# One core, sixteen sequences through two transformer blocks: an explicit turn for every piece of work, one copy for the values, and a mask term on another engine

## The reference

```
# block 0 (per sequence)
x = x + Wo·attention(q,k,v of LN(x), mask_self)            # 16 heads of 16
x = x + Wc·attention(q of LN(x), k,v of ctx, mask_cross)
x = x + W2·gelu(W1·LN(x))
# attention: scores = (q·k)/4 * mask - 10000*(1 - mask); softmax; times v
# block 1 (per sequence): recurrent mixing, 32 heads of 8
xn = LN(x); sx = shift(xn) - xn; five mixed streams from a low-rank tanh
w = exp(-exp(...)); per token: s = k v^T + w*s; out = r·(u k v^T + s)
x = x + (groupnorm(out) * silu(g))·Wo
x = x + sigmoid(r2) * relu(k2)^2·Wv
```

## Time and profile before

| | |
|---|---|
| time, median of 3 runs | 693.77 us (692.63 to 694.01) |
| span of the profiled execution | 694.0 us |
| PE busy | 645.3 us (93%) |
| DVE busy | 598.2 us (86%) |
| ACT busy | 571.7 us (82%) |
| POOL busy | 311.6 us (45%) |
| mean granted TensorE clock | 0.985 |

### The profile page before, as it was taken

One profiled execution on the slowest core, in us unless ns is written; L12 is line 12 of the kernel. 1 busy time (PEld: TensorE's weight loads), 2 busy tenths in 40 slices (PEclk: granted clock), 3 DMA queues, 4 the chain that ended last, 5 costly groups with the idle time before them and its releaser, 6 DMA issues.

```text
span 694.0 us, 17297 instructions
## 1 busy us (share of the span) xinstructions
PE 645.3 (93%) x5877; PEld 561.6 (81%) x5877; DVE 598.2 (86%) x1430; ACT 571.7 (82%) x2071; POOL 311.6 (45%) x440
## 2 busy tenths in 40 slices
PE   6878998999999999999999999999999989898776
PEld 5666787888989888988989888989888877687555
DVE  3598588999999999999999999999999987968274
ACT  1568899899999999999999999999999987664513
POOL 1154252646464554636364646454554624432120
PEclk9999999999999999999999999999999999999799
DMA  8920031221305050504122231305050503120200
GB/s 306 325 70 9 2 104 36 70 70 58 88 9 138 1 146 1 145 2 122 25 85 62 67 81 53 93 4 144 1 146 1 146 0 108 31 70 0 69 9 8
DMA packets 53725, 50.44 MB, mean 73 GB/s; under 512 B 6030, under 2 KB 48902, under 8 KB 53254
## 3 DMA queue, kind: packets, MB, share of 16 engines
q1 hardware_dynamic: 53638, 49.34, 24.7%
HBM read 28.62 MB, written 3.93 MB: 47 GB/s over the span
## 4 chain that ended last, share of the span: by engine, by line
PE 80%; DVE 8%; ACT 7%; issue 3%; POOL 1%; DMA 0%; SPq 0%; DVEq 0%; ACTq 0%; POOLq 0%
PE PS_B L552 16%; PE PS_T L654 9%; PE PS_B L694 8%; PE PS_S L552 7%; PE PS_D L559 5%; PE PS_S L625 4%; PE PS_T L662 4%; PE PS_S L559 4%; PE PS_T L559 4%; ACT SC L1291 3%; PE PS_D L800 2%; PE PS_B L703 2%; PE PS_D L552 2%; ACT PT L1301 2%; PE PS_T L545 2%
## 5 line engine op out<-in xcount | busy, mean ns | idle before, releaser
L1291 ACT ACTIVATE SC<-SC,NMX 128x128 f32<-128x128 f32 x512 | 200.0, 398 | 0.2
L1291 ACT ACTIVATION_READ_ACCUMULATOR SC<-SC,NMX 128x1 f32 x512 | 101.0, 197 | 0.0
L654 PE MATMUL PS_T<-CST,SC 128*128 128x128 f32 x512 | 81.3, 281 | 7.7 <-ACT PT L1301 3.6
L976 DVE TENSOR_REDUCE NMX<-SC 128x4 f32<-128x512 f32 x128 | 85.2, 676 | 0.4 <-POOL SC L1499 0.3
L1301 ACT ACTIVATE PT<-PS_T 128x512 f32<-128x512 f32 x120 | 70.8, 590 | 12.7 <-PE PS_T L654 12.7
L654 PEld LDWEIGHTS PS_T<-CST,SC 128*128 128x128 f32 x512 | 56.4, 141 | 26.1 <-ACT PT L1301 12.7
L1057 DVE TENSOR_TENSOR_SCAN SS<-W,AJ 128x1024 f32<-128x1024 f32 x32 | 73.2, 2288 | 0.2
L552 PE MATMUL PS_B<-MX,W 128*128 128x128 f32 x512 | 64.2, 280 | 4.7 <-ACT KR L1350 4.7
L552 PEld LDWEIGHTS PS_B<-MX,W 128*128 128x128 f32 x512 | 61.3, 196 | 4.9 <-ACT KR L1350 4.9
L1499 POOL TENSOR_TENSOR SC<-SC,MADD 128x512 f32<-128x512 f32 x48 | 59.9, 1276 | 6.5 <-DVE SC L956 6.5
L552 PE MATMUL PS_B<-B_LT,W 128*128 128x128 f32 x512 | 61.1, 278 | 1.0 <-ACT B_LT L1231 0.9
(11 more groups left out here) (231 smaller groups left out, 1595.0 us busy)
## 6 DMA issues: line engine op xcount, KB each, us to landing
W<-EW SPq DMA_DIRECT2D x32, 512.0 KB, 4.1
V<-values_by_head SPq DMA_DIRECT2D x28, 512.0 KB, 5.4
W<-in_weights SPq DMA_DIRECT2D x1, 4160.0 KB, 21.0
ENC<-in_enc SPq DMA_DIRECT2D x16, 128.0 KB, 2.3
out<-X SPq DMA_DIRECT2D x16, 128.0 KB, 5.8
X<-in_x SPq DMA_DIRECT2D x1, 1920.0 KB, 15.7
values_by_head<-VC SPq DMA_DIRECT2D x14, 128.0 KB, 1.8
W<-in_weights SPq DMA_DIRECT2D x1, 1280.0 KB, 8.5
```

The lines of the kernel that those rows point to most:

```text
L654: last = pe.transpose(PS_T[:, j * T:(j + 1) * T], SC[:, nr(b, a) % 2, g, j, :], ident)
L976: dve.tensor_reduce(NMX[:, nr(b, a) % 2, GH * g:GH * g + GH], SC[:, nr(b, a) % 2, g], AX_X, ALU.max, negate=True)\
L1291: last = act.activation(SC[:, nr(b, a) % 2, g, j, :], SC[:, nr(b, a) % 2, g, j, :], ACT.Exp, bias=NMX[:, nr(b, a) % 2, h:h + 1], accum_out ...
```

## The change

1. `run` no longer walks a list cycle by cycle. Each entry has a turn number in ten-thousandths of a cycle (TURN = 10000); a piece of sequence b has the place TURN*b + turn, and each engine's pieces are sorted by it. A second table per engine (`PE_MOVED`, ...) gives single sequences of a piece a turn of their own. So every engine's order is new, and it need not repeat from one sequence to the next.
2. `a_val` copies both halves by one ACTIVATE through a strided view, `halves(n)`.
3. `a_lessmask` moves from ACT to POOL, as a `tensor_scalar` with multiply and add.

How far the orders move, by comparing the lists: of PE's 800 pieces 565 keep their place and the mean shift is 0.4 places (9 at most); of DVE's 1408, 465 keep it, mean shift 1.8 (24 at most); of ACT's, mean shift 1.9 (35 at most); of POOL's, 2.6. On SP the stores of the results come two cycles later than before, behind the DMAs of the decays and values.

```diff
-    ("d_final", 0, 6), ("a_addmask", (0, 0), 1), ("b_addnorm", 0, 4), ("b_addnorm", 1, 4), ("b_addnorm", 2, 4),
...
+    ("a_root", 0, 4880), ("a_addmask", (0, 0), 9189), ("a_addbias", 0, 13591), ("a_addmask", (0, 2), 14279),
+    ("a_lessmask", 0, 20510), ("a_root", 1, 22743), ("a_addbias", 1, 24972), ("a_addmask", (1, 0), 25421),
...
+def in_order(order, moved):
+    turns = [(TURN * b + moved.get((name, arg), {}).get(b, turn), name, arg, b)
+             for name, arg, turn in order for b in range(B)]
+    return [(name, arg, b) for _, name, arg, b in sorted(turns, key=lambda t: t[0])]
...
+        def halves(n):
+            whole = VP[:, n]
+            return bass.AP(whole.tensor, whole.offset, [whole.ap[0], [4 * HD, NH // 2], [3 * HD, 2], [1, HD]])
...
-        def run(pieces, order, i):
-            for name, arg, lag in order:
-                if 0 <= i - lag < B:
-                    pieces[name](i - lag, arg)
+        def run(pieces, order, moved):
+            for name, arg, b in in_order(order, moved):
+                pieces[name](b, arg)
...
-                v = values.rearrange("p (h q d) -> p h q d", q=2, d=HD)
-                for q in range(2):
-                    last = act.activation(VP[:, nr(b, a) % 2, :, q, q * HD:(q + 1) * HD], v[:, :, q, :], ACT.Copy)
-                last.then_inc(a_v, 1)
+                act.activation(halves(nr(b, a) % 2), values.rearrange("p (h q d) -> p h q d", q=2, d=HD), ACT.Copy)\
+                    .then_inc(a_v, 1)
...
-            def a_lessmask(b, _):
-                if not later(b):
-                    act.wait_ge(in_rest, IN_REST)
...
-                act.activation(MADD[:, b % 2, :], MASK[:, b, :], ACT.Copy, bias=-10000.0, scale=10000.0)\
-                    .then_inc(a_less, 1)
...
+            def a_lessmask(b, _):
+                if not later(b):
+                    pool.wait_ge(in_rest, IN_REST)
+                if b > 1:
+                    pool.wait_ge(a_added, nth(POOL_ADDS, b - 2, max(POOL_ADDS)))
+                    pool.wait_ge(a_dadded, nth(DVE_ADDS, b - 2, max(DVE_ADDS)))
+                pool.tensor_scalar(MADD[:, b % 2, :], MASK[:, b, :], 10000.0, -10000.0, ALU.mult, ALU.add)\
+                    .then_inc(a_less, 1)
```

More of the change, by code:

```diff
@@ L84 @@
     ('d_keyrec', 0, 15): 4, ('d_val', 0, 15): 2}
+TURN = 10000
 SP_ORDER = [
-    ("b_vspread", 0, 4), ("d_store", 0, 6), ("b_wspread", 0, 3), ("b_vstore", 0, 3), ("a_load", 0, 0)]
-PE_ORDER = [
[L90 to L99, removed]
@@ L133 @@
-POOL_ORDER = [
-    ("d_final", 0, 6), ("a_addmask", (0, 0), 1), ("b_addnorm", 0, 4), ("b_addnorm", 1, 4), ("b_addnorm", 2, 4),
[L135 to L140, removed]
+    ("a_load", 0, 90000), ("b_wspread", 0, 110004), ("b_vstore", 0, 110008), ("b_vspread", 0, 120002),
@@ new lines @@
+    ("d_store", 0, 170032),
+]
+SP_MOVED = {
+    ("b_wspread", 0): {0: 120002, 1: 110008}, ("b_vstore", 0): {0: 120004, 1: 110010}, ("b_vspread", 0): {0: 120006},
+}
+PE_ORDER = [
+    ("a_turn", 0, 5843), ("a_key", 0, 7175), ("a_val", 0, 7312), ("a_query", 0, 7959), ("a_scores", 0, 9566),
+    ("a_prob_turn", (0, 0), 14631), ("a_prob_turn", (0, 1), 15127), ("a_prob_turn", (0, 2), 16395),
+    ("a_prob_turn", (0, 3), 17781), ("a_pv", 0, 18202), ("a_out", 0, 18848), ("a_enc_turn", 0, 21658),
+    ("a_turn", 1, 22836), ("a_val", 1, 22840), ("a_key", 1, 22853), ("a_query", 1, 24031), ("a_scores", 1, 24831),
+    ("a_prob_turn", (1, 0), 30031), ("a_prob_turn", (1, 1), 30431), ("a_prob_turn", (1, 2), 30869),
+    ("a_prob_turn", (1, 3), 31941), ("a_pv", 1, 32759), ("a_out", 1, 33632), ("b_turn", 0, 35637),
+    ("b_mlp1", 0, 36073), ("b_mlp1", 1, 36146), ("b_mlp2", 0, 36404), ("b_mlp2", 1, 36683), ("b_turn", 1, 38500),
+    ("b_low1", 0, 39117), ("b_low2", 0, 39900), ("b_low2", 2, 40783), ("b_decay1", 0, 41184), ("b_decay2", 0, 42100),
+    ("b_keyrec", 0, 42323), ("b_keyrec", 1, 42486), ("b_valgate", 0, 42904), ("b_valgate", 1, 43283),
+    ("b_select", 0, 45549), ("b_select", 1, 47217), ("d_own", 0, 50300), ("d_read", 0, 50797), ("d_oturn", 0, 51376),
+    ("d_biasout", 0, 54348), ("d_yturn", 0, 54513), ("d_out", 0, 55700), ("d_turn", 0, 56741), ("d_keyrec", 0, 58705),
+    ("d_keyrec", 1, 58719), ("d_val", 0, 59317),
+]
@@ new lines @@
+POOL_MOVED = {
+    ("a_root", 0): {0: -50000, 1: -59990, 2: 5538, 3: 652, 5: 4997, 7: 2352},
+    ("a_addmask", (0, 0)): {0: -49998, 2: 8108}, ("a_addbias", 0): {0: -49992, 1: -59988, 9: 14995},
+    ("a_addmask", (0, 2)): {0: -49994, 1: 15526, 2: 9355, 6: 10056, 7: 12906, 12: 14995, 13: 12533},
+    ("a_lessmask", 0): {0: -49986, 1: -59982, 9: 24376, 10: 15423}, ("a_root", 1): {1: 18561, 5: 19462, 12: 22496},
+    ("a_addbias", 1): {8: 25030, 11: 33028}, ("a_addmask", (1, 0)): {0: 26196, 1: 20675},
+    ("a_addmask", (1, 1)): {0: 26462}, ("b_root", 0): {0: 30654, 2: 34999, 15: 32995}, ("b_shift", 0): {14: 38378},
+    ("b_addnorm", 0): {3: 39434, 14: 38404, 15: 38842}, ("b_addnorm", 1): {3: 39515, 14: 38685, 15: 38844},
+    ("b_addnorm", 2): {3: 39732, 5: 44672, 10: 42381, 14: 38687, 15: 38902}, ("d_rstate", 0): {13: 48396},
+    ("d_root", 0): {13: 54981}, ("d_final", 0): {10: 62628, 12: 60981},
+}
@@ L519, in _ @@
             pieces = named(a_load, b_vstore, b_vspread, b_wspread, d_store)
-            for i in range(B + LAG):
-                run(pieces, SP_ORDER, i)
+            run(pieces, SP_ORDER, SP_MOVED)
             sp.wait_ge(stored, 16 * B)
@@ L864, in _ @@
                            d_own, d_read, d_oturn, d_yturn, d_biasout, d_out, d_turn, d_keyrec, d_val)
-            for i in range(B + LAG):
-                run(pieces, PE_ORDER, i)
+            run(pieces, PE_ORDER, PE_MOVED)
         @block.vector
@@ L1216, in _ @@
                            d_moments, d_mixed, d_mixing)
-            for i in range(B + LAG):
-                run(pieces, DVE_ORDER, i)
+            run(pieces, DVE_ORDER, DVE_MOVED)
         @block.scalar
@@ L1450, in d_keyrec @@
                 act.activation(RR[:, :], rec, ACT.Tanh, scale=0.5).then_inc(d_rr, 1)
-            pieces = named(a_enc_copy, a_lessmask, a_scale, a_val, a_key, a_exps, a_prob_copy, a_widen, a_spread,
+            pieces = named(a_enc_copy, a_scale, a_val, a_key, a_exps, a_prob_copy, a_widen, a_spread,
                            b_scale, b_gelu, b_low, b_decay1, b_keyrec, b_decay2, b_decays, b_values,
                            b_gatetanh, d_first_states, d_own, d_ocopy, d_squares, d_root_of, d_root, d_affine, d_scale, d_keyrec, d_relu2)
-            for i in range(B + LAG):
-                run(pieces, ACT_ORDER, i)
+            run(pieces, ACT_ORDER, ACT_MOVED)
         @block.gpsimd
@@ L1566, in d_final @@
                 pool.tensor_tensor(X[:, b, :], RR[:, :], X[:, b, :], ALU.add).then_inc(d_fin, 1)
-            pieces = named(a_root, b_shift, d_shift, d_final, a_addbias, a_addmask, b_root, b_addbias, b_addnorm,
+            pieces = named(a_lessmask, a_root, b_shift, d_shift, d_final, a_addbias, a_addmask, b_root, b_addbias, b_addnorm,
                            d_rstate, d_gates, d_root)
-            for i in range(B + LAG):
-                run(pieces, POOL_ORDER, i)
+            run(pieces, POOL_ORDER, POOL_MOVED)
 def kernel(**inputs):
```

202 lines of the change are left out of this document (168 added, 34 removed), and 3 rows, old and new, of the table PE_MOVED.

## The result

The changed kernel takes 686.40 us (685.11 to 687.06), the kernel before beside it 693.89 (692.63 to 694.44): ratio 0.9897, 95% interval 0.9877 to 0.9917. It is faster by about 7.1 us by the ratio and 7.5 by the medians, where 12 were forecast. The profiled executions have spans of 694.0 and 685.3 us, 8.7 apart.

The account below looks back on a forecast made before the run. It took matmuls to bound the middle, with DVE close behind, and chains of short steps the ends. From 694.0 us, -4.5 - 3 - 2.5 - 2 = -12.0 gave 682.0 us, range 670.5 to 692.0.

Parts of the forecast that it names:

- step 3: Order from 646 to 694 us: two table loads fewer and KR earlier start the last recurrence's product sooner; -4.5 us.
- slow clock: At the end, PE finishes v and gate at 652.5 us with a fast clock, 654.3 with the slow one.
- step 4: Order from 540 to 646 us: other matmuls fill PE's waits for the layer norm; -3 us, bounds 0 and -9.3.
- step 5: Order from 0 to 140 us: scores issued ahead of the waiting output projection; -2.5 us, bounds +1.6 and -8.
- step 6: Order in the middle: gain only where a copy was late for PE's weight loads; -2 us.
- steps 1 and 2: Values by one copy, 0.06 us saved per pair, and mask term on POOL: 0 on the time.
- The hold-up weighed there: POOL and DVE slow each other when running together; POOL's shift took 1.75 us instead of its mean 0.68.
- worst case for the mask term: Sixteen new POOL instructions hold DVE, or are held, for at most 4.8 us in all.
- A: Rival: only the end comes, fills elsewhere merely move gaps; -4.5 and -1, 688.5 us; chance 0.18.
- B: Rival: more gain, middle 9 us, start 6, 540 to 646 us 4, end 4.5; 670.5 us; chance 0.14.
- C: Rival: in the middle DVE waits for OW and becomes the bound; slower, 697.3 us; chance 0.10.
- D: Rival: the end gives 4.5 us and the cycle's loss elsewhere cancels it; about 693.5 us; chance 0.06.

Follow-up runs that it names:

- the tail alone: Kernel before with the new order of ACT, PE, DVE and POOL only in the last 50 us: 688.56 us, ratio 0.9916.
- after: The changed kernel, with the new order throughout and both edited operations, against the kernel before: 686.40 us, ratio 0.9897.
- operations: Kernel before, its order kept, with only the one strided values copy and the mask term on POOL: 694.69 us, ratio 1.0014.
- both tails: Two kernels before with new order only at the end: on ACT, PE, DVE and POOL, 688.56 us; on ACT alone, 690.21 us.
- both ends: Kernel before with the new order in the first 130 and last 50 us, old middle and old operations: 689.14 us, ratio 0.9922.
- the order alone: The changed kernel's new order with the old values copies and the mask term on ACT: 687.47 us, ratio 0.9910 to the kernel before.
- the repeated changed kernel: The changed kernel run once more, unaltered, for comparison on the same chip: 686.49 us, ratio 0.9885 to the kernel before.
- ACT's tail: Kernel before with the new order in the tail on ACT only; PE, DVE and POOL as before: 690.21 us, ratio 0.9951.

## Why the prediction was right in its sign and 4 us off in its size

**The end (step 3): right mechanism, term mis-sized.** -4.5 was taken. From the decays' inner exponentials to the product 7.1 us came (16.05 to 9.0), and the order of the tail alone gives 5.3 of the 7.5 us by medians. Of the 2.6 us between 4.5 and 7.1, 1.0 lies ahead of KR and 1.6 behind it.

Ahead of KR, the forecast had the square of 14 at 646.85 and the decays behind it, so that KR starts 3.5 us behind the 646.24 of the decays. But in the new order PE turns OH of 14 ahead of the last decay matmuls, at 642.77 instead of 644.92. The square ran at 644.82, where ACT waited for PE, and left the chain; KR starts 2.5 us behind the decays. (The "1.8 us earlier" compares KR's end at 650.3 with its old start; from start to start the forecast is 2.4.)

Behind KR, it kept PE's slow clock as one of two cases for v and the gate. They took 1.16 and 1.06 us in after (651.11 - 650.05 for the second) instead of 3.78; PE had waited 1.28 us and not 4.75, and the granted clock was 1.00 and not 0.50. That is some 1.6 us of the 7.1. And it had the select done at 656.6 at the earliest, while it was done at 654.5. Its -4.5 puts the product at 657.8, 8.1 us behind its KR; it came 6.5 behind. The forecast of 10 to 12 us from the decays to the product came out at 9.0.

The loads were priced rightly by the trace. From the decays to KR it takes 5.87 us before and 2.49 after, 3.4 less. What left this stretch is two loads (2.6), and a square, a root and a one-element instruction (0.9): 3.5. After, a load starts at 646.72 and lasts 1.28, and the next instruction starts at 648.01, 0.01 us behind its end.

**540 to 646 us (step 4): failed.** The B_N waits fell from 4.6 to 1.3, more than forecast, yet MX of sequence 12 to MX of sequence 15 takes 106.0 us before and 106.1 after. Both profiles have a fall of the clock near 563 us, to 0.50 for 3.4 us; those with the old order and none there (operations, both tails, both ends) take 103.5 to 105.6, and the order alone 104.9. So no gain shows at an equal clock either. The fillers moved the wait to SC and KK. "What is filled in would have run in another gap" was the lower bound of the term, and is what happened: 0 instead of -3.

**The start (step 5): at most 0.8 us came, and most of it was given back.** -2.5 was taken. MX of sequence 1 comes 1.1 us earlier in this profile, but in the repeated changed kernel it comes at 130.6, no earlier than before, since MX of sequence 0 itself moves between 92.2 and 93.6 from one profile to the next, whichever the start. From MX of 0 to MX of 1 it takes 36.8 to 36.9 us with the new start and 37.7 with the old; from 1 to 2 it takes 0.15 us more, with both ends 0.6. From MX of 0 to MX of 12 the changed kernel takes 446.8 and 447.2 us, before 447.2. Against it stands a fall of the clock to 0.50, for 3.4 or 6.8 us from between 26 and 29 us on, which all six profiles with the new start have; of the eight with the old one only "operations" has a fall in the start, at 38 us. So PE's 2.7 us more of busy time by 140 us is not all more work (1075 records against 1061). The stretch in before, then in after:

```profile
26.00:35.00 9.00, 8.07 (x85) 6.27 (x86) 3.98 (x11) 3.86 (x16) 0.00 (x0) 1.00 0.78 212
```
```profile
26.00:35.00 9.00, 7.28 (x32) 6.32 (x33) 3.05 (x8) 4.16 (x14) 1.29 (x3) 0.62 0.83 227
```

**The middle (step 6): failed, with its premise.** "The middle is bound by the matmuls themselves" was read from 398.63 of 400 us. Without 14.5 us of them the turn is the same. A busy share doesn't say that less work would shorten the turn: ends of matmuls are modelled, and with less PE work the chain runs through ACT and is as long. So -2 for earlier copies had nothing to work on; the turn is 0.04 us longer, 0.07 in the repeated kernel and 0.12 in the order alone.

**The two operations (steps 1 and 2): right.** 0 was counted, and -0.3 to +2.2 us is the interval of the operations alone. The strided copy takes 0.388 us against 0.44 for the pair, near the -0.06 forecast; the mask term takes the 0.298 us of the earlier trace rows. DVE's maxima wait for POOL's adds 1.7 us in all after and 0.3 before, but 1.8 in "both ends", which has the mask term on ACT: the order of the start makes that wait. The hold-up weighed there shows both ways in the kernel before: POOL's shift took 1.75 us beside DVE's product, where its median is 0.61, and the product at 147.16 us took 1.45, where its median is 1.22, beside a TENSOR_SCALAR of POOL (L1526) that ran for 0.62 us from 146.93. The shift takes 0.61 in each of its 16 turns after, 0.61 in the order alone too, and again 1.75 once with the old cycle of "both ends": in after and in the order alone no shift runs beside such a product. The 4.8 us of the worst case for the mask term did not come.

**The rivals.** A, only the end comes, is what happened, with an end bigger than A's: 4.5 + 1 forecast, 7.1 measured, 686.4 instead of 688.5. B fell with the middle. C fell at the turn of 37.26 us (37.4 was its mark): with `d_own@7` moved forward DVE waits for OW 1.4 us in the whole run, before 2.2. D fell, as at most 0.5 us was given back. The median lies inside the range because an end 2.6 us too small stood beside three guessed terms, -7.5 of the -12.0, of which at most 0.6 us came. The total was 4.4 us off only because the two errors have opposite signs, and that is luck.

## What to carry to other kernels

In a tail, follow one chain instruction by instruction and reorder for it: more than one engine's order had a part here (ACT's 4.0 us, the others' 2.8), and most of it arrived (MX-AJ 6.8 us in the tail alone, median 5.3; the profile lost 1.4 of it to the clock). In a full cycle, a wait that a filler removed was followed by the next one and gave nothing here; before pricing such fills, relieve one engine in an experiment and look at the turn. And compare executions at an equal granted clock. An engine at 99.7% busy isn't shown to be the bound until less work for it makes the turn shorter.

## What the hardware showed

- The clock in the tail: the same instructions from AJ to FIN take 28.07 us, or about 29.15 to 29.8 when the granted clock is down over four matmuls 7 us behind AJ (for after and the tail alone, 1.00 and 0.61 from 662 to 665 us).
- Executions of one kernel differ by their mean clock: before takes 690.64 to 691.99 us at 0.990 and 695.29 to 695.96 at 0.985. AJ-FIN alone makes 1 to 2 us of this; the clock falls at up to four other places.
- A shorter wait paid twice: with PE idle 1.28 us, 16 matmuls of v and gate took 2.2 us, with 2.34 us idle (ACT's tail) 2.05, and with 4.75 us idle 3.78. From MX to AJ the granted clock is 0.79 in all six profiles with the old order of ACT and 1.00 in all eight with the new one.
- From 140 to 540 us an exponential over 64 columns takes 343 ns, over 128 it takes 399 (before): halving the columns of the most frequent instruction saves 14%. The read of the accumulator behind it stays at 196 to 198 ns.
